# Row maxima of the scores in groups of four heads, over five PSUM banks, with the engines' order tables laid anew

## The reference

```python
Q, K, V = heads(x @ Wq.T + bq), heads(x @ Wk.T + bk), heads(x @ Wv.T + bv)   # 16 heads of 8
scores = Q @ K.T / sqrt(8) - (i - j)          # for j <= i; -inf above the diagonal
out = softmax(scores) @ V                     # softmax with the row's maximum taken off
x = layernorm(x + merge(out) @ Wo.T + bo)
h = silu(x @ w1.T * s1) * (x @ w2.T * s2)     # ternary weights, 128 -> 512
h = gelu(h @ h1.T * t1)                       # 512 -> 512
h = gelu(h @ h2.T * t2)                       # 512 -> 512
x = layernorm(x + h @ w3.T * s3)              # 512 -> 128
```

## Time and profile before

| | |
|---|---|
| median of 3 runs | 764.61 us (764.49 to 766.36) |
| span of the profiled execution | 763.0 us, first to last instruction |
| PE busy | 721.0 us, 94% |
| DVE busy | 590.4 us, 77% |
| ACT busy | 551.7 us, 72% |
| POOL busy | 509.7 us, 67% |
| granted TensorE clock, mean | 0.957 of full speed |

### The profile page before, as it was taken

The page is one execution under the profiler, slowest core; times in us unless marked ns, Lnnn a source line. Parts: engine busy times, 40 slices in busy tenths (PEclk is TensorE's granted clock), DMA queues, the critical chain, the costliest instruction groups (busy, mean ns, idle before and its releaser), DMA issues.

```text
span 763.0 us, 18187 instructions
## 1 busy us (share of the span) xinstructions
PE 721.0 (94%) x5993; PEld 496.8 (65%) x5993; DVE 590.4 (77%) x2761; ACT 551.7 (72%) x876; POOL 509.7 (67%) x616
## 2 busy tenths in 40 slices
PE   4798999999999999999999999999999999999995
PEld 2576566666767666676766666676766667676663
DVE  4978588797978788796878879797878879787142
ACT  5265558768695977869596876869596786959683
POOL 4155565858577585857668585857758585868764
PEclk8566899999999999999999999999999999999997
DMA  7511310313121130313122031313112030310100
GB/s 238 170 35 32 111 46 9 133 30 121 45 108 55 45 105 17 128 37 114 51 75 78 17 133 30 120 46 111 52 64 86 17 131 21 119 33 24 25 1 29
DMA packets 56367, 54.18 MB, mean 71 GB/s; under 512 B 28048, under 2 KB 36496, under 8 KB 56272
## 3 DMA queue, kind: packets, MB, share of 16 engines
q1 hardware_dynamic: 55984, 52.92, 21.3%
...
...
## 4 chain that ended last, share of the span: by engine, by line
PE 57%; ACT 13%; DVE 12%; issue 8%; SPq 4%; DMA 3%; POOL 2%; POOLq 0%; DVEq 0%; ACTq 0%
PE ps L586 18%; PE ps L592 15%; DVE ps L964 7%; ACT pt L809 5%; PE ps L631 5%; PE ps L690 5%; PE ps L671 3%; PE ps L605 3%; ACT sg L859 3%; PE ps L699 2%; DVE m L964 2%; ACT L809 2%; PE ps L612 1%; DMA sums<-raw 1%; ACT k_hi L800 1%
## 5 line engine op out<-in xcount | busy, mean ns | idle before, releaser
L964 DVE CUSTOM_DVE_ANT_0 ps<-ps,causal 128x256 f32<-128x256 f32 (+1 forms) x928 | 297.4, 392 | 21.6 <-PE ps L634 21.4
L1108 POOL TENSOR_SCALAR_AFFINE_SELECT pt<-pt 128x512 f32<-128x512 f32 x256 | 160.6, 637 | 97.7 <-ACT pt L809 92.5
L1151 POOL TENSOR_TENSOR hlo<-hf,hhi 128x512 fp32r<-128x512 f32 x128 | 163.9, 1286 | 91.9 <-ACT hhi L894 90.4
L809 ACT ACTIVATE pt<-ps 128x768 f32<-128x768 f32 x256 | 194.7, 811 | 26.8 <-PE ps L673 24.4
L884 ACT ACTIVATE hf<-ps,vec_sb 128x512 f32<-128x512 f32 x128 | 86.2, 684 | 99.7 <-PE ps L592 99.7
L586 PE MATMUL ps<-hhi,h_hi 128*128 128x512 f32 x496 | 146.0, 415 | 0.3 <-ACT hhi L894 0.3
L592 PE MATMUL ps<-hlo,h_hi 128*128 128x512 f32 x496 | 139.5, 398 | 1.2 <-POOL hlo L1157 0.7
L964 DVE DVE_READ_ACCUMULATOR2_ANT m<- 128x1 f32 x928 | 130.4, 141 | 0.0
L592 PEld LDWEIGHTS ps<-hlo,h_hi 128*128 128x128 f32 x496 | 93.3, 188 | 28.8 <-POOL hlo L1157 6.3
L690 PE MATMUL ps<-pt,vst 128*32 128x256 f32 (+1 forms) x2048 | 106.5, 337 | 0.1
L586 PEld LDWEIGHTS ps<-hhi,h_hi 128*128 128x128 f32 x496 | 85.3, 188 | 20.5 <-ACT hhi L894 0.7
...
## 6 DMA issues: line engine op xcount, KB each, us to landing
...
den<-sums SPq DMA_DIRECT2D x128, 32.0 KB, 1.9
...
```

The source lines that it names most:

```text
L809: nc.scalar.activation(pt[u][:, c:c + 2, :], ps[:, first:last + 1, 0:3 * P], ACT.Exp).then_inc(t_free.sem, 1)
L964: part = nc.vector.tensor_tensor_reduce(ps[:, bank, cols], ps[:, bank, cols], mask, 1.0, LOWEST, ALU.add, ALU.max, m32[b][:, max_col(c + e ...
L1108: nc.gpsimd.affine_select(out=diag, in_=diag, compare_op=ALU.is_ge, fill=0.0, base=0, pattern=[[0, 2], [0, 2], [1, P]], channel_multiplier ...
L1151: nc.gpsimd.tensor_tensor(h_lo[layer % 2][:, m, :], hf[:, n % 4, :], h_hi[layer % 2][:, m, :].bitcast(F32), ALU.subtract).then_inc(hlo_rea ...
```

## The change

For the full slots (not for the filling ones) the maxima's scores are computed in groups of four heads: a step `sg` takes the place of two `s`. It issues the four 256-wide matmuls, one in each row group, and then the four 128-wide ones. The banks are no longer two fixed pairs: head h of the slot's 32 goes to bank number h modulo 5 of `(0, 1, 2, 3, 6)`, so that the attention output's bank 6 (`PVB`) takes part. `sg_full` counts groups of four, `sg_free` single heads. A group waits until the heads five before each of its own are out. Bank 6 must be free of the attention output (`raw_ready`) for the first round, and `w3h`, which also writes it, waits for the last head in it.

```diff
+        MAX_BANKS = SCORE[0] + SCORE[1] + (PVB,)
...
+        sg_full = Signal("sg_full", 2 * U)
+        sg_free = Signal("sg_free", 2 * H)
...
+        def max_bank(h):
+
+            return MAX_BANKS[h % len(MAX_BANKS)]
+
+        def wait_group_bank(eng, h, q):
+
+            n = len(MAX_BANKS)
+            if h >= n:
+                sg_free.wait(eng, q - 2, h - n + 1)
+            elif max_bank(h) == PVB:
+                raw_ready.wait(eng, q - 1, 2)
+            elif max_bank(h) in SCORE[0]:
+                t_free.wait(eng, q - 1, 2 * HP - 1)
+            else:
+                t_free.wait(eng, q - 1, 2 * HP)
+
+        def wait_heads_out(eng, bank, q):
+
+            sg_free.wait(eng, q - 2, 1 + max(h for h in range(2 * H) if max_bank(h) == bank))
...
+                        elif kind == "sg":
...
+                            for c in range(C):
+                                rows = slice(32 * c, 32 * c + 32)
+                                heads.append((max_bank(H * b + C * u + c), qs[p][rows, u, b * T:(b + 1) * T],
+                                              ks[p][rows, u, b * T:(b + 1) * T]))
+                            wait_group_bank(pe, H * b + C * u, q)
+                            wait_group_bank(pe, H * b + C * u + C - 1, q)
...
+                            for bank, qr, kr in heads:
+                                pe.matmul(ps[:, bank, 0:T], qr[:, P:T], kr, start=True, stop=False,
+                                          skip_group_check=True)
+                            for bank, qr, kr in heads:
+                                last = pe.matmul(ps[:, bank, T:T + P], qr[:, 0:P], kr[:, 0:P], start=False,
+                                                 stop=True, skip_group_check=True)
+                            last.then_inc(sg_full.sem, 1)
...
+                            if q + 2 < PAIRS:
+                                wait_heads_out(pe, W3_BANK, q + 2)
...
-                        part.then_inc(s_free.sem, 1)
+                            if q:
+                                part.then_inc(sg_free.sem, 1)
+                        if q == 0:
+                            part.then_inc(s_free.sem, 1)
```

All five order tables are new. Of each a line:

```diff
-    ("s", 1, 6, 0), ("s", 1, 7, 0), ("qq", 1), ("g", 0, -1), ("u", 0, -1), ("w3h", -2), ("st", 0, 0, 0),
+    ("x1t", -1), ("h", 2, 3, -2), ("sg", 1, 3, 0), ("g", 0, -1), ("qq", 1), ("w3h", -2), ("st", 0, 0, 0),
...
-    ("gate", 3, -2), ("arec", 0, -1), ("gmul", 3, -2), ("smax", 0, 0, 0), ("smax", 0, 1, 0), ("smax", 0, 2, 0),
+    ("arec", 0, -1), ("gate", 3, -2), ("gmul", 3, -2), ("smax", 0, 0, 0), ("smax", 0, 1, 0), ("smax", 0, 2, 0),
...
-    ("hhi", 2, 2, -2), ("hhi", 2, 3, -2), ("qhi", 0, 1), ("tanh", 0, -1), ("exp", 0, 0, 0), ("exp", 0, 1, 0),
+    ("gelu", 2, 3, -2), ("table", "exp", 0), ("hhi", 2, 3, -2), ("qhi", 0, 1), ("tanh", 0, -1), ("exp", 0, 0, 0),
...
-    ("gather", 0, 0, -1), ("gather", 0, 1, -1), ("repack", 0, 0, -1), ("repack", 0, 1, -1), ("spread", 0, 0, -1),
+    ("repack", 0, 0, -1), ("gather", 0, 0, -1), ("gather", 0, 1, -1), ("repack", 0, 1, -1), ("spread", 0, 0, -1),
```

More of the change, by code:

```diff
@@ L152 @@
-    ("exp", 1, 1, 0), ("exp", 1, 2, 0), ("tanh", 3, -1), ("exp", 1, 3, 0), ("exp", 1, 4, 0), ("exp", 1, 5, 0),
-    ("exp", 1, 6, 0), ("exp", 1, 7, 0), ("ghi", 1, -1), ("ghi", 2, -1), ("ghi", 3, -1), ("araw", 1, 0),
-    ("gelu", 1, 0, -1), ("hhi", 1, 0, -1), ("gelu", 1, 1, -1), ("hhi", 1, 1, -1), ("gelu", 1, 2, -1),
-    ("hhi", 1, 2, -1), ("table", "gelu", 0),
+    ("gelu", 1, 3, -2), ("hhi", 1, 3, -2), ("gelu", 2, 0, -2), ("hhi", 2, 0, -2), ("gelu", 2, 1, -2),
+    ("lnnorm", 1, -1), ("hhi", 2, 1, -2), ("gelu", 2, 2, -2), ("x1hi", -1), ("x1c", -1), ("hhi", 2, 2, -2),
@@ L156 @@
+    ("gelu", 1, 0, -1), ("hhi", 1, 0, -1), ("table", "gelu", 0), ("gelu", 1, 1, -1), ("hhi", 1, 1, -1),
+    ("gelu", 1, 2, -1), ("hhi", 1, 2, -1),
 ]
 DVE_ORDER = [
-    ("gate", 3, -2), ("arec", 0, -1), ("gmul", 3, -2), ("smax", 0, 0, 0), ("smax", 0, 1, 0), ("smax", 0, 2, 0),
-    ("arec", 1, -1), ("smax", 0, 3, 0), ("smax", 0, 4, 0), ("smax", 0, 5, 0), ("smax", 0, 6, 0), ("smax", 0, 7, 0),
-    ("res1", -1), ("smax", 1, 0, 0), ("lnstat", 1, -1), ("smax", 1, 1, 0), ("smax", 1, 2, 0), ("mTc", 0, 0),
@@ new lines @@
+    ("smax", 0, 3, 0), ("arec", 1, -1), ("smax", 0, 4, 0), ("smax", 0, 5, 0), ("smax", 0, 6, 0), ("smax", 0, 7, 0),
+    ("smax", 1, 0, 0), ("res1", -1), ("smax", 1, 1, 0), ("lnstat", 1, -1), ("smax", 1, 2, 0), ("mTc", 0, 0),
+    ("mTl", 0, 0), ("smax", 1, 3, 0), ("smax", 1, 4, 0), ("smax", 1, 5, 0), ("x1lo", -1), ("smax", 1, 6, 0),
+    ("smax", 1, 7, 0), ("qlo", 0, 1), ("gate", 0, -1), ("gmul", 0, -1), ("qlo", 1, 1), ("gate", 1, -1),
+    ("mTc", 1, 0), ("res2", -2), ("mTl", 1, 0), ("gmul", 1, -1), ("lnstat", 2, -2), ("gate", 2, -1),
@@ L180 @@
+    ("spread", 0, 1, -1), ("spread", 0, 2, -1), ("xload", 2), ("gather", 1, 0, -1), ("spread", 0, 3, -1),
+    ("gather", 1, 1, -1), ("repack", 1, 0, -1), ("repack", 1, 1, -1), ("spread", 1, 0, -1), ("spread", 1, 1, -1),
+    ("spread", 1, 2, -1), ("spread", 1, 3, -1), ("mTd", 0, 0, 0), ("mTd", 0, 1, 0), ("mTd", 1, 0, 0),
+    ("mTd", 1, 1, 0), ("qstack", 1), ("kstack", 1), ("store", -2), ("tload", 0),
 ]
@@ L451, in wait_exp_banks @@
                 t_free.wait(eng, 0, 2 * HP - 1 + i)
+            elif i < 2 and q == 0:
+                wait_max(s_free, eng, q, HP - 1 + i)
             elif i < 2:
-                wait_max(s_free, eng, q, (2 * HP if q else HP) - 1 + i)
+                for bank in SCORE[i]:
+                    wait_heads_out(eng, bank, q)
             else:
@@ L958, in run @@
                         u, c = n // 2, 2 * (n % 2)
-                        wait_max(s_full, dve, q, HP * b + n + 1)
+                        if q:
+                            sg_full.wait(dve, q - 2, U * b + u + 1)
+                        else:
+                            wait_max(s_full, dve, q, HP * b + n + 1)
                         if n == 0:
                             mT_full.wait(dve, q - 1, b + 1)
-                        for e, bank in enumerate(SCORE[n % 2]):
+                        for e in range(2):
+                            bank = max_bank(H * b + 2 * n + e) if q else SCORE[n % 2][e]
                             for it, cols, mask in ((1, slice(0, T), causal[:]), (0, slice(T, T + P), causal[:, P:T])):
```

34 lines of the change are left out of this document (18 added, 16 removed), and 17 rows, old and new, of the table PE_ORDER.

## The result

The changed kernel takes 779.44 us (median of 4 runs, 777.72 to 780.56); the kernel before took 765.24 us in 4 runs beside it (764.49 to 766.36). The ratio is 1.0183, 95% interval 1.0166 to 1.0200: slower by 14 us. The forecast was 770, with a range up to 778. The direction was right; the size was outside the range by 1.4 us.

A forecast was written before the change was run, and what follows sets the result against it. Bound taken as a ring of waits through SP's queue, DVE and PE, despite PE busy 721.0 of 763.0 us. Slot 43.85 against 43.34: +6.5 over 13 intervals, less about 1.0, span 768.5; median forecast 770, range 757 to 778.

The forecast's parts named there:

- Step 1: From g(0) to the maxima's transposition: SP starts the mT_hi DMAs at 7.2 us.
- Step 2: SP's queue to arec(0): 11.28 us as before plus 0.98 for `x_tok` and a repack ahead of the gathers; arec(0) at 19.45.
- Step 3: DVE's gate(3) behind arec(0) delays gmul, cast and low part; h(1,0) stalls 0.9 us, ending at 23.75.
- the walk: One slot of the changed kernel followed in six steps from g(0), claiming the next g(0) at 43.85 us.
- Steps 4 and 5: Bank hand-over and remaining maxima: sg(0,3) stalls 0.5 us for DVE, x1t 0.3 for the layer norm; done at 42.9.
- Step 6: Slot's turn: without qq's cover g(0) waits for the last gelu's bank, 43.1 + 0.7, so at 43.85.
- The sum: A slot of 43.85 us against 43.34; 13 intervals add 6.5, about 1.0 kept early: span 768.5, median 770.
- What the grouping saves: On PE, fewer runs of `s`: about 1.5 us per slot, 21 us over 14 slots if nothing else moved.
- The table load: On ACT, moved between the last gelu and its cast: 1.28 us, hidden with 0.35 to spare.
- Faster: Query stack first frees SP's queue of 0.8 us; arec(0) at 18.65, slot 43.05, 760 us; chance 0.30.
- My sign of being wrong: Wrong if arec(0) comes under 19 us after g(0), PE waits for none of three, or slot under 43.2.

The follow-up runs named there:

- e4: Kernel before (pairs of heads, four banks) with all five order tables of the kernel after, each `sg` written as two `s`: 778.85 us, ratio 1.0196.
- e12: Kernel before with two SP placements of the change: `x_tok` load behind the store, first repack ahead of the gathers: 768.28 us, ratio 1.0065.
- e2: Kernel after with SP's order undone: first repack behind both gathers, `x_tok` load ahead of the maxima's DMAs: 766.29 us, ratio 1.0021.
- e6: Kernel after with the edits of e1, e2 and e5 together: 761.6 us, ratio 0.9958.
- e8: Kernel before (pairs, four banks) with the tables of e6, each `sg` written as two `s`: 764.81 us, ratio 1.0012.
- e3: Kernel after's grouping and five banks with the order tables of the kernel before, except the `sg` placed as in the kernel after: 817.54 us, ratio 1.0698.
- e11: e6 with the load of `x` behind the second gathers and repacks, and the exp table load back behind tanh(0): 762.61 us, ratio 0.9989.
- e7: Kernel after with only the `x_tok` load moved back ahead of the maxima's DMAs: 771.46 us, ratio 1.0108.
- e1: Kernel after with gate(3) ahead of arec(0) on DVE again: 772.8 us, ratio 1.0104.
- e5: Kernel after with qq ahead of g(0) on PE again: 775.94 us, ratio 1.0152.
- e10: e8 with the shorter of each head's two row-maximum instructions left out in the full slots: 741.63 us, ratio 0.9713.
- e9: e6 with the shorter of each head's two row-maximum instructions left out in the full slots: 744.66 us, ratio 0.9753.

## Why the prediction came out as it did

**Step 1, the start of the transposition: right.** 7.2 us after g(0) was predicted; in the kernel after the first mT_hi DMA stands 6.96 after it in the mean (arec(0) at 19.73 less 12.76).

**Step 2, SP's queue: the issue part right, the landing mis-sized. This is the step that failed.** "The change puts two DMAs ahead of the gathers", 0.98 us: the issue part grew by 0.95 (9.63 to 10.58), and e4 and e12, which share SP's order, have 10.57 and 10.58. Stack DMAs in another order at nothing: right as well, since e2, e6 and e8 are at 9.5 to 9.6 with it. But I carried "and then 1.28 us to land" over unchanged, and in the kernel after it is 2.18 in the mean (1.25 to 3.04), 0.9 us more. Of these, 0.3 are the one slot that I read, whose landing is short (the mean before is 1.57). They did no harm, since its issue part is long (10.0 for a mean of 9.63): with the means of the kernel before my sum gives 19.38 instead of 19.45. The other 0.6 is growth that came with the grouping, and the sum put it at nothing without a reason. As the slot follows arec(0) one for one, it is worth 0.6 x 13 = 8 us; the span missed by 7.5. Luck covered some of it: step 1 came 0.24 early, so arec(0) was at 19.73 after g(0) and not at 20.0.

**Where the growth comes from** is open. It isn't the tables: every kernel with groups has it, e3 and e11 too (2.0 to 2.3, e7 1.8, against 1.45 to 1.6 with pairs). It isn't the bytes of `x_tok` either: with them out of the way e2 still lands in 2.08. It comes late in the run: in the kernel after the first four steady slots land in 1.25 to 1.44, the other eight in 2.08 to 3.04. Seven of these eight have a 16 KB `instruction` packet beside the landing, none of the first four has, and none of the twelve in the kernel before.

**Once the slack is gone, every late arec(0) is paid in full.** Four of the 12 slots of the kernel before (43.6 to 43.9) were already longer than the rest, three of them with arec(0) at 19.1 to 19.5. In the kernel after all twelve follow it. Four slots (43.4 to 43.8) are under the 43.85 predicted; the eight late ones, 44.2 to 46.0, make the mean of 44.46.

**Step 3, gate(3) behind arec(0): right**; e1 returns 6.6 us. From arec(0) to sg(0,1) it is 4.44 us for the 4.30 of the walk, in the quick slot and in the late one. That h(1,0) waits at its first matmul (1.40) in the late slot, and not at its last, changes nothing in that distance.

**Steps 4 and 5: right**, 0.41 for the 0.5 at sg(0,3), two waits of 0.14 that I had not listed, 0.54 for the 0.3 at x1t. **Step 6, g(0) without its cover: the wait right**, 0.40 for 0.45. But e5, which gives the cover back, leaves the ring as long as it was (31.58 for 31.57 us), and its 3.5 us less are not clear of the spread.

**The sum.** 0.61 us a slot (44.46 for 43.85) x 13 = 7.9; the span is 7.5 over the 768.5 predicted. 0.28 of the 0.61 is arec(0). 0.2 is what the walk behind it came out too short, 24.6 us from arec(0) to the next g(0) for 24.4, in early and late slots alike; 0.1 is the slot of the lower clock and the one in which `wo` waits. The other 1.9 us of the miss: the median stands 3.4 above this span, where before it stood 1.6 above, because the profiled execution is the fastest of the four.

**What the grouping saves.** PE's busy time fell by 17 us (21 predicted), in a steady slot from 42.9 to 41.9, 1.0 for the 1.5 of the sum, and my reading of what saves it was too narrow. With the row-maximum reading cut, PE is as busy with pairs as with groups (700.1 and 699.7, e10 and e9), and pairs are the faster by 3 us; with it whole, the groups save 14.5 us of PE (e8, e6), all but 3 of it in time in which DVE is the later one anyway. The Trainium skill's rule on this (TensorEngine Tiling (Array Packing), PSUM Bottleneck: tiling speeds up TensorE, and the draining of PSUM may become the bottleneck) holds here: taking 105 us of the draining away gives 17 us (e6 to e9), grouping gives 3.

**The table load: hidden, as predicted.** In the kernel after it lasts 1.28 us on the line of "table":

```profile
L887 ACT ACT_TABLE_LOAD  x17: 1283/1283/1283, 60.2 to 755.2; - x17
```

PE didn't wait for the cast behind it in the quick slot, and moving it back (e11, with one edit more) gained nothing.

**The rivals.** "Faster" needed arec(0) before 18.95 and the query stack to free the queue; it came at 19.73. What that rival priced, a slot of 43.05 and 760, is what e6 reached in ten of its 12 slots (43.03 to 43.10, 761.6 in all), by other means. My sign of being wrong, arec(0) under 19 us after g(0), shows in three of the 12 slots and not in the mean.

**Open.** Why the gathers land later with groups (above), and with it up to 8 of the 14 us. Pairs in the same tables (e4) don't have it in eleven of 12 slots and lose as much in other places: their two `s` run apart, as in e8, and it is 25.6 us from arec(0) to the next qq for 25.2. So the order remains the cause of the loss either way.
